# A couple's outputs moved from behind the second score tile to ahead of the first, in a gated cross-attention and expert kernel

## What is computed

```python
q = split_heads(layernorm(x) @ Wq + bq)          # 16 heads of 16
k, v = split_heads(ctx @ Wk + bk), split_heads(ctx @ Wv + bv)
scores = where(mask, -1e15, q k^T / 4)
x = x + tanh(g_xattn) * (softmax(scores) v @ Wo + bo)
n = layernorm(x)
probs = softmax(tanh(mean(n) @ W1 + b1) @ W2 + b2)
# per element the best 3 of 8 experts e, weights w_e from probs
x = x + tanh(g_ffn) * (n + sum_e w_e * gelu(n @ Wa[e]) @ Wb[e])
```

## Time and profile before

| | |
|---|---|
| time before, median of 3 (lowest, highest) | 325.0 us (323.65, 325.36) |
| the profiled execution | 321.64 us, span 319.8 us |
| TensorE matmuls busy | 286.0 us (89%) |
| TensorE weight loads busy | 237.7 us (74%) |
| VectorE | 226.2 us (71%) |
| ScalarE | 223.9 us (70%) |
| GpSimd | 134.6 us (42%) |
| `pv`, L1101 | 768 matmul instructions, 24 per couple |

### The profile page before, as it was taken

The page is one execution under the profiler, slowest core; times in us unless marked ns, Lnnn a source line. Parts: engine busy times, 40 slices in busy tenths (PEclk is TensorE's granted clock), DMA queues, the critical chain, the costliest instruction groups (busy, mean ns, idle before and its releaser), DMA issues.

```text
span 319.8 us, 10356 instructions
## 1 busy us (share of the span) xinstructions
PE 286.0 (89%) x3940; PEld 237.7 (74%) x3940; DVE 226.2 (71%) x642; ACT 223.9 (70%) x439; POOL 134.6 (42%) x185
## 2 busy tenths in 40 slices
PE   1709769899999999999999978999999999999996
PEld 1406547677777777777766646999999999999996
DVE  7317837667777787777879555887886777777773
ACT  2322538797787977888778785867676976866763
POOL 3501468587686887769868981000100000000000
PEclk9977979999999999999999999999999999999999
DMA  7458666786777868767594503110210011010101
GB/s 165 125 137 244 174 172 206 177 271 183 207 241 178 280 189 239 238 178 238 153 262 150 161 18 88 32 33 2 59 42 23 17 31 45 4 46 3 33 2 31
DMA packets 39457, 40.59 MB, mean 127 GB/s; under 512 B 10264, under 2 KB 35264, under 8 KB 39408
## 3 DMA queue, kind: packets, MB, share of 16 engines
q1 hardware_dynamic: 37296, 38.94, 43.4%
q10 hardware_dynamic: 1936, 0.79, 1.0%
q0 software_dynamic: 176, 0.20, 0.2%
HBM read 33.09 MB, written 6.74 MB: 125 GB/s over the span
## 4 chain that ended last, share of the span: by engine, by line
PE 62%; DMA 13%; SPq 7%; DVE 5%; issue 4%; ACT 3%; POOL 3%; DVEq 0%; ACTq 0%
PE bank L1280 16%; PE bank L1307 16%; PE bank L1119 7%; DMA qbd<-q_scr 7%; PE bank L1069 4%; PE bank L1101 4%; PE bank L1081 3%; PE bank L1085 3%; SPq L341 3%; DMA k_scr<-wb 3%; PE bank L1110 2%; PE bank L1145 1%; DMA stage<-in_L_ffn_Wb 1%; SPq L350 1%; DMA stage<-in_L_ffn_Wa 1%
## 5 line engine op out<-in xcount | busy, mean ns | idle before, releaser
L807 DVE CUSTOM_DVE_ANT_0 bank<-bank,maskb 112x375 f32<-112x375 f32 x128 | 67.8, 569 | 34.3 <-PE bank L1069 33.8
L1280 PE MATMUL bank<-ctxT,wqkvo 128*128 128x112 f16 x960 | 59.4, 213 | 2.7 <-DVE qbd L933 2.3
L1280 PEld LDWEIGHTS bank<-ctxT,wqkvo 128*128 128x128 f16 x960 | 56.5, 98 | 3.4 <-issue 3.4
L1307 PE MATMUL bank<-stage,pT 128*128 128x112 f16 x1104 | 58.1, 213 | 0.0
L469 POOL TENSOR_SCALAR stage<-stage 128x512 f32<-128x512 f32 x64 | 38.6, 621 | 43.1 <-DMA stage<-in_L_ffn_Wb 22.2
L1307 PEld LDWEIGHTS bank<-stage,pT 128*128 128x128 f16 x1104 | 55.8, 98 | 0.3
L555 ACT ACTIVATE pT<-bank 125x448 f32<-125x448 f32 x96 | 50.0, 537 | 8.3 <-PE bank L1085 7.9
L1069 PE MATMUL bank<-kst,qbd 128*112 128x375 f16 x128 | 34.4, 340 | 17.1 <-DMA qbd<-q_scr 13.9
L1280 PE MATMUL bank<-ctxT,qbd 128*128 128x112 f16 x192 | 40.8, 213 | 0.0
L474 POOL TENSOR_TENSOR wb<-stage,wb 128x512 f16<-128x512 f32 x32 | 36.7, 1168 | 3.1 <-ACT wb L665 2.7
L474 POOL TENSOR_TENSOR wa<-stage,wa 128x512 f16<-128x512 f32 x32 | 36.3, 1156 | 1.1 <-ACT wa L665 1.1
(11 more groups left out here) (134 smaller groups left out, 478.6 us busy)
## 6 DMA issues: line engine op xcount, KB each, us to landing
stage<-in_L_ffn_Wa SPq DMA_DIRECT2D x16, 512.0 KB, 4.3
stage<-in_L_ffn_Wb SPq DMA_DIRECT2D x16, 512.0 KB, 4.7
kst<-k_scr SPq DMA_DIRECT2D x64, 93.8 KB, 3.8
k_scr<-wb SPq DMA_DIRECT2D x16, 187.5 KB
ctx_s<-in_ctx SPq DMA_DIRECT2D x8, 336.0 KB
qbd<-q_scr SPq DMA_DIRECT2D x32, 56.0 KB, 3.2
xa<-in_x SPq DMA_DIRECT2D x8, 112.0 KB, 4.2
q_scr<-wb SPq DMA_DIRECT2D x16, 56.0 KB, 3.1
```

Source lines behind the costliest of these rows:

```text
L807: v.tensor_tensor_reduce(out=bank[0:SQ, e, 0:SK], in0=bank[0:SQ, e, 0:SK], in1=maskb[0:SQ, b % 2, 0:SK], scale=-1.0, scalar=FLOOR, op0=ALU ...
L1280: ins = T.matmul(o, first(ws, t, f), x2b[:, b % 2, (xs * DT + t) * SQ:(xs * DT + t + 1) * SQ], start=(t == 0 and xs == 0 and ws == 0), sto ...
L1307: ins = T.matmul(o, second(u, ws * (2 * CHUNK) + f * D + t * 128), hT[:, u % 2, hs * FT * SQ + f * SQ:hs * FT * SQ + (f + 1) * SQ], start= ...
```

## The change

In every slot the call of `pv` goes from behind the second tile to the head of the slot, ahead of the first tile. Nothing else is changed: the same couple's outputs, the same waits inside `pv`, and all other engines' lists are as before.

```diff
             for b in range(-2, B):
                 for slot in range(4):
+                    pv(b if slot else b - 1, (slot - 1) % COUPLES)
                     st_tile(b, slot, 0)
                     s1(b + 1, 2 * slot)
                     st_tile(b, slot, 1)
-                    pv(b if slot else b - 1, (slot - 1) % COUPLES)
                     uses = slot_uses(b, slot)
```

## The result

The changed kernel takes 329.75 us (median of four runs, 327.7 to 332.67) against 325.18 before. Compared with the runs of before beside it, the ratio is 1.0173, with a 95% interval of 1.0107 to 1.024; a second set of runs gave 1.0185 (1.0145 to 1.0226). So it is slower by 5.6 to 6 us; the ratios take undisturbed executions alone, which is why they say more than the 4.6 us between the two medians. Forecast were 3 us.

What follows compares the result with a forecast made beforehand. TensorE was taken as the bound, with q's DMA ending several rounds. Six rounds' growth, 3.25 us, less 0.2 at the end, gave about +3.0 on the median of 325.0: 328.0 us, range 323.8 to 330.5.

Steps and rivals of the forecast that it cites:

- The rounds shielded by a DMA: Second, fourth and sixth rounds, ended by q's DMA: growth of only +0.15, +0.2 and +0.6 us.
- The path of TensorE: Rounds ended by TensorE: +0.04 us to slot 2's transposes, +0.9 in all to the next S1 pair.
- Size of what moves, 0.78 us: Outputs 0.70 us plus 0.08 for the step into them; first tile, first S1 pair, second tile come later.
- Late loads in slots 0 and 2: Where maxima follow, two weight loads late by 0.18 us each become four; slots 1 and 3 keep two.
- the fourth rival: Late weight loads count in full: 0.72 us more per round, +4.3 over six rounds, 329.3 us; chance 0.07.
- The wait that moves: Slot's head: outputs await the previous slot's third-tile exponential; slack covers it, 0 us, at most 0.3 in slot 3.
- Rival 3: Outputs wait for their exponential in every slot, 0.2 us or more in 28 slots: +6 us, 331; chance 0.06.
- Less cover for the third tile: Slots 1 and 3: third tile stalls about 0.1 us for the first tile's exponential, ends 0 to 0.3.
- The end: Behind the seventh S1 pair: the maxima's copy has 0.24 us less idle, -0.2 us, ends -0.5 to 0.
- Rival 1: Slot 0's outputs hide in DMA waits, kernel gets faster: three stretches 0.60 us shorter each, 323.2 us; chance 0.12.
- Rival 2: No measurable difference: bank path has more room, some +1 us in all, 326.0 us; chance 0.25.

Runs made afterwards that it cites:

- e12: Changed kernel with the first S1 pair ahead of the outputs at the head of each slot; ratio to before 1.0331.
- e14: Kernel before, with the outputs at the slot's head in the last two passes only; ratio to before 1.0063.
- e13: Changed kernel, with the outputs back in the old place in the last two passes; ratio to before 1.0175.
- e5: Kernel before plus one small product of 17 weight columns per slot, between first tile and first S1 pair; ratio to before 1.0121.
- e6: Kernel before plus one small product of 128 weight columns per slot, between first tile and first S1 pair; ratio to before 1.0025.
- e7: Kernel before with the outputs moved to between the first S1 pair and the second tile; ratio to before 1.0107.
- e10: Changed kernel with the transposes of the maxima directly behind the outputs at the head of slots 0 and 2; ratio to before 1.0127.
- e1: Kernel before with the outputs moved to the slot's head in slots 1 and 3 only; ratio to before 1.0109.
- e3: The changed kernel run again without any edit; ratio to before 1.0185.
- e15: Kernel before, x2T copy ahead of slot 2's weight conversions, maxima's transposes heading slots 0 and 2 in passes up to b = 1; ratio to before 0.9857.

## Why the prediction was wrong

The sign was right, and so was the path on which the loss lies: the rounds that ended on TensorE grew. The size was half, 3.0 against about 6 us, and several steps failed.

*The rounds shielded by a DMA: the step that failed most.* In two traces of each kernel the rounds grew, on average, by 0.8, 0.7, 1.1, 1.4, 1.3 and 1.1 us where I had 0.5, 0.15, 0.9, 0.2, 0.9 and 0.6. For the second, fourth and sixth, which ended on q's DMA in the trace I had, I let the DMA's wait swallow the growth and put 0.95 us on all three; they grew by 3.2. In the second the DMA did not end the round any longer, TensorE did. In the fourth I credited 0.69 us of idle, and the changed kernel idles there for 0.69 and 0.42 again: in its first trace q's read took 5.50 us where it had taken 4.40. And that round's 20.79 us was one execution's (20.23 in the other). A slack of one round from one trace was taken for a property of the kernel, and the DMA's end for a fixed point.

*The path of TensorE.* +0.04 foreseen to L1177, +0.88 from there to the next pair, together 0.9. Measured, in rounds 4 to 6 of the changed kernel, L1177 comes 15.16 to 15.20 us behind the round's S1 pair against 14.93 to 15.08 before, about +0.2. From there to the next pair it is 6.07 in the steady ones against 4.97: +1.10. In the third round L1177 came at 15.71 in one trace and 15.31 in the other, for there the turn of the outputs waited 0.60 and 0.24 for ScalarE's copy, which stands behind the second exponential, a wait I did not follow.

*Size of what moves, 0.78 us.* The 0.70 was right. The 0.08 for the step into the outputs was read where they stood, behind a score tile. In the new place they stand behind projections and transposes, and nothing I cited shows that pair of neighbours. The load is late by 0.53 behind L1119 and 0.34 behind L1185, but only by 0.14 behind the 112-column transposes, in place of 0.18 four times. The price of a neighbour was taken from the old neighbour; over the round the errors nearly cancel.

*Late loads in slots 0 and 2.* The outputs' exit and the maxima's entry are new in both, 0.18 each, as counted. With the entries they make 0.87 us more per round, where the fourth rival had 0.72. By the Trainium skill's rule on changed tiling modes ("TensorEngine Tiling (Array Packing)", Key Properties) each change drains TensorE. The traces agree, as the load is late by 0.14 to 0.53 us, more behind matmuls of more columns. That the drain lasts as long as the matmul in flight has to run is read from this, not measured.

*The wait that moves.* Right in steady rounds, where the outputs do not wait for their exponential. It failed elsewhere: they wait 0.61 us at the head of the slot 0 that opens the second round (at 63.85), and 1.07 and 1.32 in the last two passes, of which I had said that slots 0 to 2 keep more slack. Rival 3 fell as a rule for every slot.

*Less cover for the third tile.* 0.1 us foreseen, 0.18 to 0.27 late at the load in slots 1 and 3; and VectorE's maxima, which I let run "in the same time", add 0.18 to 0.27 at the second S1 pair behind it. This term was about two times too small, and the second was put at nothing; e12 has 0.50 there with one tile less to cover.

*The end.* -0.2 foreseen; about 2 us by e14 and the traces, nothing by e13. The cause stays open.

*The rivals.* Rival 1, hiding in DMA waits: TensorE's idle for q did vanish from all but one round, and nothing was won, as the move of the maxima came no earlier (12.59 us behind the second round's S1 pair against 12.23) and the write of k neither. Rival 2 fell. Rival 4 was part of the truth: at what e5 and e6 give for a late load, 0.87 more of them per round are some 3 us over six rounds (an estimate, with a wide interval), about half of the loss. Its 329.3 us lies next to the measured median of 329.75; that is luck, for it let the late loads count in full and left out the growth of the waits. e7 puts 0.8% on the order, and e10 shows that the two do not add up freely.

One sum does not close: the second traces of the pair differ by 8.2 us in span (328.4 against 320.2), the timed runs by 6.0. Part of it is that the traced execution of before was 2.2 us faster than its median, and that of the changed kernel 0.9 slower. Which rounds differ less in the other runs can't be seen.

## What to carry to other kernels

When a block with its own tile width moves in TensorE's list, price its entry by the instruction that it will stand behind: here the same load was late by 0.14 to 0.53 us, by its neighbour. When a block leaves a gap between a product and the next user of its bank, count what else fills that gap; the cover it gave is part of its place. And a slack read in one execution of a loop should be compared over its rounds and over a second execution before it is spent in a sum; a DMA that ends a round moves with what starts it.

## What the runs showed of the hardware

A load of 17 columns came late by 0.53 us behind 375-column float32 matmuls, 0.34 behind 256-column ones, 0.28 behind an S1 pair (375 columns, float16), 0.18 behind a score tile and 0.14 behind 112-column float32 transposes.

In three profiled executions with the new order in the last passes (the first of the changed kernel, e1 with half of the outputs moved, and e14) the granted clock of TensorE fell to its lower level of 1.2 GHz for some microseconds at the end of the attention stage. Stretches of the changed kernel (columns as in the earlier trace rows):

```profile
195.00:198.00 3.00, 0.96 (x13) 0.70 (x17) 0.72 (x1) 3.00 (x8) 3.00 (x3) 1.00 0.01 3
...
202.00:204.00 2.00, 2.00 (x28) 1.26 (x23) 1.47 (x4) 0.10 (x1) 0.00 (x0) 0.50 0.90 264
```

Ahead of it TensorE was busy 0.96 of 3 us. From 197.83 to 206.44, from one couple's outputs to the last, the changed kernel needs 8.6 us. In e3, where the clock did not fall (TensorE busy 1.26 of the 3 us from 193 to 196), the same stretch takes 6.4, from 197.53 to 203.96; before, from 188.99 to 194.62, it was 5.6. In e14 the clock was 0.70 from 194 to 198. So about 2 us of that stretch in the first trace are the clock's. The clock also fell to 0.50 for some 3 us behind the S1 pair that opens the first round, in fourteen of the seventeen traces, of before and changed alike, and stayed high there in e10, e12 and e15; in e10 and e15 TensorE's idle ahead of it was 1.25 and 1.13 us in place of 2.77, in e12 it was 2.85, so a shorter idle is not the only thing that keeps it high.
